# A two-layer decoder in one program: the preparation ahead of attention reordered, value products moved into the first attention turns

## What is computed

```python
# A: latent self-attention of layer 0 (16 heads, causal, rope on 64 of 128)
kv = h @ wkv_a; kv_c, k_pe = kv[..., :64], kv[..., 64:]
kv_dec = rms_norm(kv_c, kv_norm_w) @ wkv_b        # k_nope, v per head
scores = (q_nope . k_nope + rope(q_pe) . rope(k_pe)) * 128 ** -0.5
x = x + (softmax(mask(scores)) @ v) @ out_proj_w
# X: latent cross-attention to ctx (16 heads, window of 9 keys by seg_id)
kv_c = ctx @ W_kvc; q_c = h @ W_dq                # no rms norm here
scores = (q_nope . (kv_c W_uk) + rope(q_c W_qr) . rope(kv_c W_kr)) / sqrt(192)
x = x + (softmax(window(scores)) @ (kv_c W_uv)) @ W_o
# then: top-4 of 32 experts, a state-space layer, a wkv recurrence, a quantised FFN
```

## Time and profile before

| | us |
|---|---|
| three runs | 851.47, 854.07, 857.70; median 854.07 |
| the profiled execution | 851.53, span 849.8 |
| busy in the span: TensorE, VectorE, ScalarE, POOL | 691.2, 673.0, 529.5, 496.6 |

### The profile page before, as it was taken

How to read it: one execution, slowest core, us unless ns; L and a number is a source line. 1 busy time by engine, 2 the same in 40 slices (tenths; PEclk the granted TensorE clock), 3 DMA queues, 4 the chain that set the end, 5 groups by cost and what they waited for, 6 DMA issues and landing times. The chain is left out here.

```text
span 849.8 us, 22555 instructions
## 1 busy us (share of the span) xinstructions
PE 691.2 (81%) x8286; PEld 521.7 (61%) x8289; DVE 673.0 (79%) x1500; ACT 529.5 (62%) x1439; POOL 496.6 (58%) x528
## 2 busy tenths in 40 slices
PE   4899999999999989359999707988889888951464
PEld 3578888888888767159899603335555555541333
DVE  6867777898888977568788557779889998879957
ACT  2644555556556655247667594579899787209287
POOL 2057777777878776045555177117899898624211
PEclk9999999999999999669999957999999999985779
DMA  7827000000000320017875543022333342000001
GB/s 303 274 88 310 1 1 2 7 1 8 1 7 8 123 91 14 7 54 201 235 218 148 112 122 99 2 82 75 110 118 103 103 172 105 6 1 0 1 13 38
DMA packets 30347, 71.44 MB, mean 84 GB/s; under 512 B 5472, under 2 KB 19488, under 8 KB 28320
## 3 DMA queue, kind: packets, MB, share of 16 engines
q1 hardware_dynamic: 25680, 57.54, 19.1%
q0 software_dynamic: 4560, 12.46, 6.3%
HBM read 59.57 MB, written 10.42 MB: 82 GB/s over the span
## 5 line engine op out<-in xcount | busy, mean ns | idle before, releaser
L1921 POOL TENSOR_TENSOR arena<-arena 128x1024 f32<-128x1024 f32 x63 | 147.2, 2372 | 29.6 <-DVE arena L1860 23.3
L1860 DVE TENSOR_TENSOR_SCAN arena<-arena,ps 128x1024 f32<-128x1024 f32 x64 | 142.1, 2270 | 14.7 <-ACT arena L1730 7.5
L1548 PEld LDWEIGHTS ps<-arena 64*64 64x64 f32 x4096 | 79.3, 134 | 65.4 <-DVE arena L1860 26.0
L1548 PE MATMUL ps<-arena 64*64 64x64 f32 x4096 | 91.8, 222 | 19.1 <-issue 9.4
L647 PE MATMUL ps<-arena 128*128 128x128 f32 (+1 forms) x768 | 101.1, 282 | 0.9 <-PEq L376 0.9
L647 PEld LDWEIGHTS ps<-arena 128*128 128x128 f32 (+1 forms) x768 | 91.6, 193 | 14.3 <-issue 13.1
L852 ACT ACTIVATE arena<-arena 128x128 f32<-128x128 f32 x256 | 98.8, 389 | 1.2 <-DVE arena L776 1.1
L1088 POOL DMA_INDIRECT arena<-tokens,arena x63 | 60.6, 962 | 58.6 <-PE ps L1124 41.8
L860 ACT ACTIVATE arena<-ps 128x512 f32<-128x512 f32 x64 | 38.2, 597 | 86.8 <-PE ps L666 86.8
L907 POOL TENSOR_TENSOR arena<-arena 128x512 f32<-128x512 f32 x64 | 66.6, 1041 | 22.1 <-DVE arena L782 22.1
L1557 PE MATMUL ps<-arena 64*64 64x512 f32 x544 | 72.8, 595 | 2.2 <-POOL arena L1921 0.8
(11 more groups left out here) (322 smaller groups left out, 1517.3 us busy)
## 6 DMA issues: line engine op xcount, KB each, us to landing
arena<-c_rows SPq DMA_DIRECT2D x32, 512.0 KB, 3.7
arena<-in_E_gu SPq DMA_DIRECT2D x8, 1024.0 KB, 12.9
expert_out<-arena SPq DMA_DIRECT2D x63, 128.0 KB
arena<-in_E_dn SPq DMA_DIRECT2D x1, 4096.0 KB, 13.4
arena<-in_ctxT SPq DMA_DIRECT2D x2, 1024.0 KB, 5.6
arena<-in_A_o SPq DMA_DIRECT2D x1, 2048.0 KB, 16.0
arena<-in_X_o SPq DMA_DIRECT2D x1, 2048.0 KB, 22.0
arena<-in_F_w SPq DMA_DIRECT2D x4, 512.0 KB, 5.9
```

Source lines behind the costliest of these rows:

```text
L1548: t = eng.matmul(psD[d][cols, k, at:at + R], dtuT[rows, b, c, cols], diagB[rows, i % 2, b, :], start=True, stop=True)
L1860: eng.tensor_tensor_scan(hst[s % 4], dA[s % 4], psD[s % 2].rearrange("p k m -> p (k m)"), 0.0, ALU.mult, ALU.add).then_inc(h_ready, 1)
L1921: eng.tensor_tensor(hC[s % 4], hst[s % 4], Csb[i % 4], ALU.mult).then_inc(hC_ready, 1)
```

## The change

In the preparation TensorE, ScalarE and VectorE do A's norm and keys first and X's keys behind them. The norm's turns to hT come before the first absorbing product. The rms roots of A are taken per token: the squares are the stationary operand, so the sums come out with tokens on partitions, eight columns; one Sqrt and one reciprocal of 128x8; then the identity scaled by them (`rms_diag`, 2 x 128x512 on VectorE) is summed by a product with ones (`pe_key_rows`), which gives the row of inverse roots 64 times, and ScalarE copies it to SBUF (`act_key_rows`). X's sine product and sum move to POOL (`key_rope`, with a scratch of its own, keytmpX); the three wide mask steps of VectorE move behind A's keys. ctxT has memory of its own, so that it need not be read before h is written. A's value products leave the preparation and take turns 0 to 3 of the attention, X's take turns 5 to 8, all four copies of each by ScalarE. Loads: x comes third, A's query columns ahead of X's absorbing weights, X's value and output weights last; the attention block starts when A's query columns are there, the others are waited for in its turns.

```diff
-        def act_key_root(eng, K, half):
-            eng.wait_ge(K.ssq, half + 1)
-            eng.activation(keytmp[0:R, half, :], ps[0:R, half, :], ACT.Sqrt, bias=rms_eps[0:R, :],
+        def act_key_root(eng, K):
+            eng.wait_ge(K.ssq, 2)
+            eng.activation(rms_root, ps[:, 0, 0:2 * NB].rearrange("p (b k) -> p b k", k=2)[:, :, 0], ACT.Sqrt, bias=rms_eps,
                            scale=1.0 / R).then_inc(K.root, 1)
...
         def pe_key_ssq(eng, K, half):
             eng.wait_ge(K.sq, half + 1)
-            eng.matmul(ps[0:R, half, :], ones[0:R, 0:R], keytmp[0:R, half, :], start=True, stop=True).then_inc(K.ssq, 1)
+            for j in range(NB // 2):
+                b = half * (NB // 2) + j
+                t = eng.matmul(ps[:, 0, 2 * b:2 * b + 2], keytmp[0:R, half, j * P:(j + 1) * P], ones[0:R, 0:2],
+                               start=True, stop=True)
+            t.then_inc(K.ssq, 1)
+
+        def pe_key_rows(eng, K, half):
+            eng.wait_ge(K.diag, half + 1)
+            eng.matmul(ps[0:R, half, :], ones[:, 0:R], rms_diag[:, half].rearrange("p b t -> p (b t)"),
+                       start=True, stop=True).then_inc(K.rows, 1)
...
+        def dve_key_inverse(eng, K):
+            eng.wait_ge(K.root, 1)
+            eng.reciprocal(rms_inv, rms_root).then_inc(K.inv, 1)
+            eng.wait_ge(K.inv, 1)
+            for half in range(2):
+                four = slice(half * (NB // 2), (half + 1) * (NB // 2))
+                eng.tensor_tensor(rms_diag[:, half], ident.unsqueeze(1).to_broadcast([P, NB // 2, P]),
+                                  rms_inv[:, four].unsqueeze(2).to_broadcast([P, NB // 2, P]), ALU.mult).then_inc(K.diag, 1)
...
             @block.scalar
             def _(eng):
                 normA.act(eng)
                 eng.wait_ge(s_const, 13)
                 for half in range(2):
                     act_key_square(eng, keysA, half)
+                act_key_root(eng, keysA)
+                absorbed(0)
+                for half in range(2):
+                    act_key_latent(eng, LX, keysX, half)
+                for half in range(2):
+                    act_key_rows(eng, keysA, half)
                 absorbed(1)
                 for half in range(2):
-                    act_key_root(eng, keysA, half)
-                act_key_tokens(eng, LX, keysX, 5)
+                    act_key_place(eng, LA, keysA, half, latent=True)
...
+                act_key_tokens(eng, LA, keysA, 0)
                 for half in range(2):
-                    act_key_place(eng, LA, keysA, half, latent=True)
-                act_key_tokens(eng, LA, keysA, 3)
+                    act_key_place(eng, LX, keysX, half)
+                act_key_tokens(eng, LX, keysX, 5)
...
+                eng.wait_ge(kr_ready, 1)
+                eng.wait_ge(s_const, 6)
+                normA.pe(eng)
+                loaded(eng, "kvA")
+                for half in range(2):
+                    eng.wait_ge(normA.hT_ready, 2 * half + 2)
+                    pe_key_raw(eng, LA, keysA, hT, half)
                 loaded(eng, "absA")
                 absorb(0)
...
                 for half in range(2):
                     pe_key_ssq(eng, keysA, half)
-                pe_key_tokens(eng, LX, keysX, 5, 4)
+                loaded(eng, "ctx", "kvX")
+                for half in range(2):
+                    pe_key_raw(eng, LX, keysX, ctxT0, half)
+                for half in range(2):
+                    pe_key_rows(eng, keysA, half)
+                absorb(1)
                 loaded(eng, "absX")
...
-                for n in range(4):
-                    pe_vo(eng, "A", n, VO_BANK[n]).then_inc(vo_done, 1)
-                pe_key_tokens(eng, LA, keysA, 3, 2)
-                loaded(eng, "qA", "qX", "gate")
+                pe_key_tokens(eng, LA, keysA, 0, 2)
+                pe_key_tokens(eng, LX, keysX, 5, 4)
+                loaded(eng, "qA")
...
+        ALONE, VO_AT = 12, {"A": 0, "X": 5}
...
-                    if t < 4:
-                        if t == 0:
-                            loaded(eng, "voX")
-                        else:
-                            eng.wait_ge(voX_out, t)
-                        pe_vo(eng, "X", t, BANK_O["X"]).then_inc(voX_done, 1)
+                    for name in "AX":
+                        n = t - VO_AT[name]
+                        if 0 <= n < 4:
+                            if n:
+                                eng.wait_ge(vo_out[name], n)
+                            else:
+                                loaded(eng, "vo" + name)
+                            pe_vo(eng, name, n, BANK_O[name]).then_inc(vo_done[name], 1)
+                    if t == VO_AT["X"]:
+                        eng.wait_ge(vo_out["A"], 4)
+                        loaded(eng, "qX")
...
-                    if t < 4:
-                        dst, src = vo_pair("X", t, BANK_O["X"])
-                        eng.wait_ge(voX_done, t + 1)
-                        eng.activation(dst, src, ACT.Copy).then_inc(voX_out, 1)
+                    for name in "AX":
+                        n = t - VO_AT[name]
+                        if 0 <= n < 4:
+                            dst, src = vo_pair(name, n, BANK_O[name])
+                            eng.wait_ge(vo_done[name], n + 1)
+                            eng.activation(dst, src, ACT.Copy).then_inc(vo_out[name], 1)
```

More of the change, by code:

```diff
@@ L165, in decoder @@
         keytmp = view(o, 1024, "p (e t) -> p e t", e=2)
+        ctxT0 = view(K0, 2048, "p (c t) -> p c t", c=DC)
+        rms_diag = view(K0 + 2048, 1024, "p (e b t) -> p e b t", e=2, b=NB // 2)
+        keytmpX = view(K0 + 3072, 1024, "p (e t) -> p e t", e=2)
+        rms_root, rms_inv = roots[:, 0], roots[:, 1]
         class Norm:
@@ L267, in __init__ @@
                 self.inv = sem(tag + "_key_inv")
+                self.diag = sem(tag + "_key_diag")
+                self.rows = sem(tag + "_key_rows")
+                self.rows_in = sem(tag + "_key_rows_in")
                 self.placed = sem(tag + "_key_placed")
@@ L289, in pe_key_tokens, with dve_key_turn @@
             t.then_inc(K.tok_done, 1)
-        def dve_key_rope(eng, L, K, half):
+        def dve_key_turn(eng, L, K, half, tmp):
             ts, t4 = half_of[half], "p (b t) -> p b t"
-            raw, own, swapped = ps[R:P, K.banks[half], :], L["key"][R:P, 0, ts], keytmp[R:P, half, :]
+            raw, own, swapped = ps[R:P, K.banks[half], :], L["key"][R:P, 0, ts], tmp[R:P, half, :]
             eng.wait_ge(K.raw, half + 1)
@@ L297, in dve_key_rope, with key_rope @@
                               L["cos"][R:P, 0, :].unsqueeze(1).to_broadcast([R, 4, P]), ALU.mult).then_inc(K.parts, 1)
+        def key_rope(eng, L, K, half, tmp):
+            ts, t4 = half_of[half], "p (b t) -> p b t"
+            own, swapped = L["key"][R:P, 0, ts], tmp[R:P, half, :]
             eng.wait_ge(K.parts, 2 * half + 1)
@@ L380, in _ @@
                 load(eng, "krX", wkr[0:R, :], a["X_kr"])
+                load(eng, "x", x, a["x"])
                 load(eng, "kvX", LX["wkv"][:, :, 0:R], a["X_kvc"])
@@ L392, in _ @@
                 load(eng, "absA", kbT, a["A_kbT"])
+                for c in range(DC):
+                    load(eng, "qA", LA["wq"][:, c].rearrange("p (q e) m -> p q (e m)", e=2)[:, :, R:P + R],
+                         a["A_qr"][:, c])
                 load(eng, "absX", wuqT, a["X_uqT"])
@@ L396, in _ @@
                 load(eng, "voA", wo["A"], a["A_o"])
+                load(eng, "qX", LX["wq"][0:QC, 0].rearrange("p (q e) m -> p q (e m)", e=2)[:, :, R:P + R], a["X_qr"])
+                load(eng, "qX", LX["wdq"], a["X_dq"])
+                load(eng, "qX", gate_w, a["E_gate"])
+                load(eng, "qX", gate_b, a["E_gate_b"])
                 load(eng, "voX", wvT["X"], a["X_vT"])
                 load(eng, "voX", wo["X"], a["X_o"])
[L399 to L405, removed]
             @block.gpsimd
@@ L431, in _ @@
                 normA.pool(eng)
+                loaded(eng, "ropeX")
+                for half in range(2):
+                    key_rope(eng, LX, keysX, half, keytmpX)
             @block.vector
@@ L514, in _ @@
                 t.then_inc(kr_done, 1)
-                loaded(eng, "ctx", "kvX")
-                eng.wait_ge(kr_ready, 1)
-                eng.wait_ge(s_const, 6)
-                for half in range(2):
-                    pe_key_raw(eng, LX, keysX, ctxT0, half)
                 def absorb(c):
```

76 lines of the change are left out of this document (25 added, 51 removed).

## The result

| | us |
|---|---|
| kernel before, four runs | 851.47, 852.55, 854.07, 857.70; median 853.31 |
| changed kernel, four runs | 862.95, 863.14, 865.06, 866.12; median 864.10 |
| ratio | 1.012, interval 1.0085 to 1.0154 |
| profiled executions, before and after | 851.53 (span 849.8), 862.95 (span 861.2) |

The change costs 10.8 us (7.3 to 13.1), where 3.2 were forecast, and its median lies just above the range. The attention ends, by TensorE's first bf16 product behind it, at 351.92 us before and at 362.51 after: 10.6 of the span's 11.4 us are lost by then, so the search can stay in the first 350 us.

What follows compares the result with a forecast made beforehand. TensorE was taken to bound the attention, a chain from x's landing the start. Start -3.2, moved value products +4.1 and output stall +2.3 gave +3.2: 851.53 becomes 854.7, or 857.3 on the median's scale; range 851.5 to 863.

Steps and rivals of the forecast that it cites:

- The start: Everything before the first attention turn: first query at 39.2 us against 42.40, a gain of 3.2 us.
- I leave the cost as before: Half clock from the idle stretch ahead of the turns: 1.6 us lost, assumed the same after the change.
- Early x: In the start, x issued third instead of eighth: landing taken at 7.65 us instead of 12.18.
- Root detour: In the start, root, reciprocal and diagonal ready at 27.5, just before the rows' product at 27.65; hidden, at most 1.3 us.
- rival (5): In the start, the roots' detour comes 3 us late, so no gain there: +6.4 us, 860.5; chance 0.08.
- Value products in turns 5 to 8: X's four value products, moved to turns where TensorE is full: 1.02 us each, 4.1 us in all.
- The stall at output: In turns 5 to 8, output waits for mixed behind ScalarE's copy: about 0.55 us a turn, 2.3 in all.
- Rival (2): In turns 5 to 8, no stall at output: +0.9 us, 855.0; chance 0.10.
- The loads: New load order costs nothing: output weights of A and X's loads land with about 10 us of slack or more.
- rival (4): In the start, short-packet loads delay X's absorbing weights, first query at 45.1: +9.1 us, 863.2; chance 0.08.
- Rival (1): The clock does not fall: first turn saves 1.6 us, transposes 1.0; +0.6 us, 854.7; chance 0.20.
- Rival (3): In the start, clock stays low behind the transposes, A's raw keys at half: +1.8, together +5.0 us, 859.1; chance 0.08.

Runs made afterwards that it cites:

- e3: Changed kernel with the value products put back (A's in the preparation, X's in turns 0 to 3) and other banks for X's absorbing product: ratio 0.9996.
- e7: Changed kernel with sums of squares over 64 columns instead of 2 and the value product's copy behind mixed: ratio 1.0016 to the kernel before.
- e8: e3 with sums of squares over 64 columns instead of 2: ratio 0.9951 to the kernel before, 0.9954 when repeated.
- e9: e8 with the loads issued in the order of the kernel before (x eighth): ratio 1.0019 to the kernel before.
- e1: Changed kernel with ScalarE's copy of the value product behind mixed instead of ahead of it: ratio 1.0053 to the kernel before.
- e2: Changed kernel with sums of squares per token over 64 columns of ones instead of 2: ratio 1.0089 to the kernel before.
- e5: Changed kernel run once more, unedited, for its scatter and a second profile: ratio 1.0102 (1.0073 to 1.013) to the kernel before.

## Why the prediction was wrong

The profiled difference to the end of attention is 10.6 us: first query +1.83, first query to turn 4's transposes +0.2, four turns 4 x (6.57 - 4.76) = +7.24, and +1.3 from the stretch of half clock at 328 us, which lasted longer than before. Of the 8.2 us by which the profiled 862.95 lies above the forecast 854.7, the start has 5.0, the turns 1.0, that stretch 1.3, and 0.8 come behind the attention.

- **The start, forecast -3.2, found +1.8; against the second profile of before -1.1.** The step that failed is the pricing of the clock: "Raw keys of X 3.70: 27.65", X's absorbing product at "some 3 us", and "I leave the cost as before". Half clock was priced only where the one profile of before had it. The new order has it in two other places. X's raw keys took 3.0 us more, the sums per token 2.2 instead of 1.1, partly at half clock too, and the rows' product began at 31.10 instead of 27.65. Behind it X's absorbing product took 1.4 more than 2.93 and the token transposes 0.75 more (1.97 against 1.22 of e3), and ScalarE, the last in the chain, waited 1.64 us for them. These 3.5 and 1.6 make up the 5.0 us between the forecast 39.2 and the measured 44.23.
- **The engine work of the start** was right in sum, partly by luck. At full clock (e7) the rows' product began at 27.67, forecast 27.65, but the sums per token cost 1.9 there and not 1.1 (22.16 to 24.04), which the earlier start of the transposes and their neighbours made up. Its first query, 40.94, holds two waits of ScalarE behind the second stretch of half clock; without them it would stand at 39.15 (estimate, 40.94 - 1.40 - 0.39), where 39.2 was forecast:

```profile
37.35 0.65 ACT L528 ACTIVATE arena<-ps 96x256 f32<-96x256 f32 x2 [1.40 <-PE ps L573]
38.39 0.60 ACT L367 ACTIVATE arena<-ps 128x512 f32<-128x512 f32 x1 [0.39 <-PE ps L303]
```

- **Early x, estimated at 7.65: right** (7.21), and nearly all of it reached the first query: 4.4 us at VectorE's start were worth 4.15 (e8 against e9).
- **Root detour: right**, the rows' product did not wait for it, in e7 with X's raw keys at 3.70 too; rival (5) fell.
- **Value products in turns 0 to 3, nothing: right** (+0.2).
- **Value products in turns 5 to 8, 4 x 1.02 = 4.1: mechanism right, size a little short**: e1 shows 1.16 each, 4.6.
- **The stall at output, 2.3: right in place and order** (released by mixed), 2.6 by e1. Rival (2) fell.
- **The loads: right**; rival (4) had the right total for a wrong reason. SP's issues of A's query columns and of the next load took 4.17 and 3.38 us, not 19.2, and nothing waited.
- **Rival (1), full clock: fell** in the changed kernel.
- **Rival (3)** fell in the first profile, where A's raw keys took 3.60 directly behind the transposes. It was not empty: they took 4.41 in the second profile and 4.65 in e2, 0.8 and 1.05 of the 1.8 us it priced. The Trainium skill's rule (TensorE: Matmul & The Clock Gate, Part 4: PE-mode transpose), that full clock doesn't engage for transposes, is not what these float32 transposes show: in the kernel before the granted clock was 0.68 in 22.5 to 23.0 after 0.50, behind more than 3 us in which TensorE did nothing but transpose, and the raw keys behind took 3.70.
- **The stretch at 328 us** was in no term: 6.8 us instead of 3.4, 1.3 us more.
- **The base.** The profiled execution of before was a favourable one: its half-clock stretches in the start were 3.4 us each, the second profile had 10.2 and 3.4. The rows of one execution can't tell a fixed term from one that differs between executions.

## What to carry to other kernels

Before moving work into a pipelined loop, ask which engine is full there and what stands behind each new instruction in its own queue: four products of 1.0 us cost 7.2 here, 2.6 of them because an in-order engine waited at the wrong place, which one exchange of two statements gives back. Work that seems to prolong a stage can be cover: with 3.7 us of products more in it, and banks that spare a wait, the preparation was 2.0 us shorter, TensorE had no gap in it, and the second fall of its clock did not come. Where a profile shows a stretch of half clock, take a second profile before using its length as a term.

## What was not expected of the hardware

- Products with two columns were hardly quicker than the same with 64: 16 records took 1.90 us at full clock (e5) against 1.95 (e7), and 2.08 to 2.25 in the four profiles in which the clock fell while they ran.
- Up to the first turns the stretches of half clock lasted 3.4, 6.8, 10.2 or 13.7 us, and one and the same kernel had different lengths in two executions.
- The granted clock shown was 1.00 in 13.4 to 17 us, though the sixteen transposes took 3.7 to 3.8 us there and 2.81 with filler ahead of them. By their durations they ran slowly behind the idle time, and the column doesn't show it.
- POOL took 1.26 us for an operation of 64x512 (four, 29.27 to 34.7 us), more than the 0.69 of VectorE's, and hid all of it.
